# LayerNorm and tanh-weight FFN on 8 cores: square root moved from ScalarE to Newton steps on VectorE, weight loads issued one by one

## What is computed

```python
def _L0_attn_ref(x):                       # x: (1, 8192, 4096); b = 1
    q = jnp.transpose(x, (2, 0, 1))
    scores = jnp.einsum('lnc,lmc->lnm', q, q) / scale
    prob = jax.nn.softmax(scores, axis=-1) # over an axis of length 1: all ones
    msg = jnp.einsum('lnm,lmc->lnc', prob, q)
    return x + jnp.transpose(msg, (1, 2, 0))

x = x + _L0_attn_ref(_layernorm(x, axis=-1))
w_b = aa * jnp.tanh(kk * weight)           # weight: (4096, 4096)
x = x + jnp.einsum('bsi,oi->bso', _layernorm(x, axis=-1), w_b) + bias
```

## Time and profile before

| | us |
|---|---|
| timed runs | 626.97 and 639.13, median 633.05 |
| profiled execution | 626.53 |
| its span, slowest core | 625.0 |
| PE busy | 494.1 (79%) |
| ACT busy | 210.8 (34%) |
| DVE busy | 150.2 (24%) |
| chain that ended last | DMA 49%, PE 23%, ACT 9% |

### The profile page before, as it was taken

How to read it: one execution, slowest core, us unless ns; L and a number is a source line. 1 busy time by engine, 2 the same in 40 slices (tenths; PEclk the granted TensorE clock), 3 DMA queues, 4 the chain that set the end, 5 groups by cost and what they waited for, 6 DMA issues and landing times.

```text
span 625.0 us, 6936 instructions; the slowest of 8 cores (608.6 to 625.0 us)
## 1 busy us (share of the span) xinstructions
PE 494.1 (79%) x2335; PEld 230.9 (37%) x2379; DVE 150.2 (24%) x336; ACT 210.8 (34%) x228; POOL 83.5 (13%) x118
## 2 busy tenths in 40 slices
PE   3033467554388999999999957998999599989993
PEld 3021133231244444444444423443444244434441
DVE  0800245631882211120023003200230023022111
ACT  0255577763544433045004521352023312330000
POOL 0001000020001120212020302020202021212111
PEclk9556686688598999999999987999999989999998
DMA  7948846389654689999989999999877997899843
GB/s 192 287 163 247 290 172 242 126 189 301 236 131 102 190 229 228 233 285 288 228 152 285 278 196 236 241 257 251 141 221 218 239 276 220 223 280 207 171 94 80
DMA packets 47699, 134.72 MB, mean 216 GB/s; under 512 B 5680, under 2 KB 5680, under 8 KB 46640
## 3 DMA queue, kind: packets, MB, share of 16 engines
q0 software_dynamic: 16416, 43.00, 35.2%
q1 hardware_dynamic: 20016, 50.37, 24.4%
q10 hardware_dynamic: 11232, 40.90, 21.5%
HBM read 117.47 MB, written 16.78 MB: 215 GB/s over the span
## 4 chain that ended last, share of the span: by engine, by line
DMA 49%; PE 23%; ACT 9%; issue 5%; ACTq 5%; DVE 4%; POOL 2%; SPq 1%; DVEq 0%; POOLq 0%
DMA wring<-w2d 26%; PE ps_acc L323 20%; DMA outs<-biasrow 11%; DMA rb<-x 7%; ACT wp L235 6%; DMA xs<-x 5%; PE ps_tr L300 3%; ACT h2T L257 3%; ACTq L225 2%; ACTq L217 2%; POOL outs L354 1%; POOL wring L342 1%; DVE outs L148 1%; DVE stats L160 1%; ACT L246 1%
## 5 line engine op out<-in xcount | busy, mean ns | idle before, releaser
L323 PE MATMUL ps_acc<-wp,h2T 128*128 128x512 bf16 x2004 | 456.0, 388 | 46.0 <-ACT wp L235 31.2
L323 PEld LDWEIGHTS ps_acc<-wp,h2T 128*128 128x128 bf16 x2048 | 203.3, 100 | 296.6 <-issue 67.7
L235 ACT ACTIVATE wp<-wring,kk_sb 128x1024 bf16<-128x1024 f32 x128 | 141.1, 1141 | 266.2 <-DMA wring<-w2d 245.3
L148 DVE SCALAR_TENSOR_TENSOR outs<-rb,s1a,ps_acc 128x512 f32<-128x512 f32 x64 | 47.8, 747 | 350.5 <-DMA rb<-x 259.3
L354 POOL DMA_DIRECT2D outs<-biasrow x64 | 56.4, 1069 | 269.7 <-DVE outs L152 259.3
L300 PE MATMUL ps_tr<-ident_sb,h2b 128*128 128x128 bf16 x256 | 31.1, 280 | 46.1 <-DVE h2b L196 33.4
L342 POOL DMA_DIRECT2D wring<-w2d x50 | 28.6, 606 | 265.7 <-ACT wp L235 250.3
L160 DVE BATCH_NORM_STATS2 stats<-xs 128x6 f32<-128x512 f32 x64 | 38.7, 679 | 32.2 <-DMA xs<-x 32.2
L300 PEld LDWEIGHTS ps_tr<-ident_sb,h2b 128*128 128x128 bf16 x256 | 21.1, 121 | 57.8 <-issue 54.6
L257 ACT CAST h2T<-ps_tr 128x512 bf16<-128x512 f32 x64 | 34.2, 585 | 19.4 <-PE ps_tr L300 18.8
L152 DVE TENSOR_SCALAR outs<-outs,b1a 128x512 f32<-128x512 f32 x64 | 31.8, 497 | 5.3 <-issue 0.4
(11 more groups left out here) (20 smaller groups left out, 24.3 us busy)
## 6 DMA issues: line engine op xcount, KB each, us to landing
wring<-w2d ACTq DMA_DIRECT2D x78, 512.0 KB, 8.1
wring<-w2d POOLq DMA_DIRECT2D x50, 512.0 KB, 6.5
xs<-x SPq DMA_DIRECT2D x8, 2048.0 KB, 12.4
rb<-x SPq DMA_DIRECT2D x64, 256.0 KB, 9.2
outs<-biasrow POOLq DMA_DIRECT2D x64, 256.0 KB, 9.0
y<-outs SPq DMA_DIRECT2D x64, 256.0 KB, 7.4
ident_sb<-ident SPq DMA_DIRECT2D x1, 32.0 KB, 2.9
kk_sb<-kk SPq DMA_DIRECT2D x1, 0.5 KB, 2.3
```

The source lines that it names most:

```text
L148: vector.scalar_tensor_tensor(outs[g % 4][:, :], rbb[g % 4][:, :], s1a[:, t:t + 1], ps_acc[g % 4][:, :], ALU.mult, ALU.add)
L235: scalar.activation(wp[ot % 2][:, jop * WPC:(jop + 1) * WPC], wr[:, sl * WPC:(sl + 1) * WPC], AF.Tanh, bias=0.0, scale=kk[:, :]).then_inc( ...
L323: mm = tensor.matmul(ps_acc[g % 4][:, :], h2T[:, t * D + ic * 128: t * D + (ic + 1) * 128], wp[ot % 2][:, ic * 512:(ic + 1) * 512], start= ...
```

## The change

The square root leaves ACT. DVE forms 1/sqrt(v) itself: a first value 1/(0.5 + 0.5 v) and two Newton steps, all on columns of 128x1. ACT no longer takes part before h2b, and `s_sc` counts two steps a tile, not three. DVE gets two waits that ACT's turn gave before: ahead of the scalars until ACT has normalized its half of the tile before, and ahead of h2b until the transposes of the tile before are done. Independent of this, ACT drains after every tanh and issues the load for the freed slot at once; `flush_w` is gone.

```diff
--- before.py
+++ after.py
@@ -103,7 +103,7 @@
         sync.dma_start(xs[1][:, :], x_h[128:256, :]).then_inc(s_xin[1], 16)
 
         def load_x(t):
-            sync.wait_ge(s_sc, 3 * (t - 2) + 3)
+            sync.wait_ge(s_sc, 2 * (t - 2) + 2)
             sync.wait_ge(s_v, 4 * (t - 2) + 4)
             sync.dma_start(xs[t % 2][:, :], x_h[t * 128:(t + 1) * 128, :]).then_inc(s_xin[t % 2], 16)
 
@@ -163,9 +163,19 @@
             vector.bn_aggr(mv[:, 0:2], stats[:, 48 * p:48 * p + 48])
             vector.drain()
             vector.tensor_scalar(sc[:, 1:2], mv[:, 1:2], EPS, None, ALU.add).then_inc(s_v, 1)
-            vector.wait_ge(s_sc, 3 * t + 1)
+            vector.drain()
+            vector.tensor_scalar(sc[:, 0:1], sc[:, 1:2], 0.5, 0.5, ALU.mult, ALU.add)
+            vector.drain()
             vector.reciprocal(sc[:, 2:3], sc[:, 0:1])
             vector.drain()
+            for _ in range(2):
+                vector.tensor_scalar(sc[:, 3:4], sc[:, 2:3], sc[:, 2:3], sc[:, 1:2],
+                                     ALU.mult, ALU.mult)
+                vector.drain()
+                vector.tensor_scalar(sc[:, 3:4], sc[:, 3:4], -0.5, 1.5, ALU.mult, ALU.add)
+                vector.drain()
+                vector.tensor_mul(sc[:, 2:3], sc[:, 2:3], sc[:, 3:4])
+                vector.drain()
             vector.tensor_scalar(s1a[:, t:t + 1], sc[:, 2:3], 2.0, 1.0, ALU.mult, ALU.add)
             vector.scalar_tensor_tensor(b1a[:, t:t + 1], mv[:, 0:1], -2.0, sc[:, 2:3],
                                         ALU.mult, ALU.mult)
@@ -187,12 +197,16 @@
                 vector.drain()
             vector.tensor_mul(sc[:, 3:4], sc[:, 2:3], aa[:, :])
             vector.drain()
+            if t > 0:
+                vector.wait_ge(s_sc, 2 * t)
             vector.tensor_mul(sc[:, 6:7], s1a[:, t:t + 1], sc[:, 3:4])
             vector.scalar_tensor_tensor(sc[:, 7:8], mv[:, 0:1], -1.0, s1a[:, t:t + 1],
                                         ALU.mult, ALU.mult)
             vector.drain()
             vector.tensor_mul(sc[:, 7:8], sc[:, 7:8], sc[:, 3:4]).then_inc(s_v, 1)
             vector.drain()
+            if t > 0:
+                vector.wait_ge(s_trT, 8 * t)
             vector.tensor_scalar(h2b[:, 0:1024], xs[p][:, 0:1024], sc[:, 6:7],
                                  sc[:, 7:8], ALU.mult, ALU.add).then_inc(s_v, 1)
             vector.tensor_scalar(h2b[:, 1024:2048], xs[p][:, 1024:2048], sc[:, 6:7],
@@ -218,15 +232,6 @@
                              w_h[ot * 128:(ot + 1) * 128, j * WPC:(j + 1) * WPC]).then_inc(s_wl[sl], 16)
             wl[0] = w + 1
 
-        pend = [0]
-
-        def flush_w():
-            if pend[0]:
-                scalar.drain()
-                for _ in range(pend[0]):
-                    issue_w()
-                pend[0] = 0
-
         def tanh_batch(ot, lo=0, hi=NTO):
             for jop in range(lo, hi):
                 w = ot * NW + jop
@@ -235,16 +240,11 @@
                 scalar.activation(wp[ot % 2][:, jop * WPC:(jop + 1) * WPC],
                                   wr[:, sl * WPC:(sl + 1) * WPC],
                                   AF.Tanh, bias=0.0, scale=kk[:, :]).then_inc(s_wp, 1)
+                scalar.drain()
                 if sl < 3:
-                    pend[0] += 1
-                    if pend[0] == 3:
-                        flush_w()
-            flush_w()
+                    issue_w()
 
         def tile_block(t):
-            scalar.wait_ge(s_v, 4 * t + 1)
-            scalar.activation(sc[:, 0:1], sc[:, 1:2], AF.Sqrt).then_inc(s_sc, 1)
-            scalar.drain()
             scalar.wait_ge(s_v, 4 * t + 2)
             if t > 0:
                 scalar.wait_ge(s_trT, 8 * t)
@@ -289,9 +289,9 @@
                 elif k == 2:
                     tensor.wait_ge(s_v, 4 * t + 4)
                 elif k == 4:
-                    tensor.wait_ge(s_sc, 3 * t + 2)
+                    tensor.wait_ge(s_sc, 2 * t + 1)
                 elif k == 6:
-                    tensor.wait_ge(s_sc, 3 * t + 3)
+                    tensor.wait_ge(s_sc, 2 * t + 2)
                 trg = trg_ctr[0]
                 if trg >= 2:
                     tensor.wait_ge(s_evT, trg - 1)
```

## The result

The changed kernel takes 645.44 us (median of 11 runs, 642.49 to 650.94), the kernel before 631.34 in the same runs. The ratio is 1.025, 95% interval 1.021 to 1.029: slower, where 610 and a gain of 16 us were forecast. The profiled execution took 645.33 us, on its slowest core, core 4, a span of 643.8.

A forecast was written before the change was run, and what follows sets the result against it. The head was taken as bound by ACT's per-tile loop, with the PE idle, the tail by a loop through GpSimd. From 626.5 us, 13.7 + 1.5 - 0.3 + 1.5 = 16.4 came off, giving 610.1, range 602 to 617.

The forecast's parts named there:

- 28.0 forecast: Head, tiles 2 and 3: two tiles at 14.0 us each instead of 37.85 together, 9.9 us won.
- as taken: Batch 0 of tanh in the head: 1.5 us won, bounds 0.5 lost to 4 won.
- 110 and 138 forecast: Signs in the head: first bias accumulation at about 110 us, statistics of tile 5 at about 138.
- DVE's new waits: Head: waits before the last scalars and h2b give the old order's guarantee; cost 0.
- rival A: Head: x loads of tiles 3 and 4 replace the square root as limit, time 618; chance 0.18 together with rival D.
- rival D: Head: the square root was not on the path, only waits change place, 625; chance 0.18 together with rival A.
- The head terms: Head: 13.7 us won in tiles 1 to 3, 1.5 in batch 0, 0.3 lost in tile 5.
- one for one: Head: whatever brings the tanh at 123.33 us forward brings tile 5 forward equally; that tanh was to start 13.7 earlier.
- Tile 5 pays about +0.3 us: Head, tile 5: 1.9 us more DVE work for the root, less 1.68 us of waiting removed.
- 0.25 us won a block, 1.5 in all: Tail's tanh bursts: earlier weight issues against added drains, between -2 and +2 us for each of six blocks.
- the stretch from there to the last matmul keeps its length, give or take 10 us: Tail, from tile 7's first transposes on: length unchanged within 10 us, while those transposes come 15 us earlier.
- Rival B: Tail: earlier weight loads lengthen bias accumulations and rb reloads, 4 us in each of six blocks, 24 lost, 634; chance 0.08.

The follow-up runs named there:

- root only: Changed kernel with the kernel before's gathered weight issues (three loads behind one drain), so only the square root's move and its waits are new; 648.36 us, ratio 1.047.
- bias rows: Bias given as 128 equal rows instead of one row read 128 times: root only 587.78 us, full change 584.39, kernel before 602.95.
- the issues alone: Kernel before with a drain and one weight issue after each tanh, square root still on ACT; 611.03 us, ratio 0.986.
- full kernel: The whole change, square root on DVE and weight loads issued one by one, against the kernel before; 645.44 us, ratio 1.025.
- the one root at the end: One square root of a constant, read by nobody, added after ACT's last tanh: root only 619.35 us, ratio 0.975; full change 605.37 us, ratio 0.950.
- the moved row: Root only with the bias in row 37 of 64 equal rows, still read 128 times; 620.01 us, ratio 0.975.
- the four-core run: Root only launched on four cores, meant as one of each pair but numbered 0 to 3 in the profile; 643.9 us.

## Why the prediction was wrong

**Right, with sizes.** The mechanism of the head held: the root off ACT shortens its loop. Two tiles take 27.0 us (28.0 forecast). Batch 0 on ACT ran from 39.2 to 65.6, 26.4 us against 27.9: 1.5 won, as taken. The first bias accumulation came at 103.9 and tile 5's statistics at 134.5 (110 and 138 forecast). DVE's new waits cost nothing: tile 2's scalars waited 18.73 us for ACT and its h2b 5.12 us for the transposes, and it was still written by 75.8, where the PE wanted it at 82.07. The statistics of tiles 3 and 4 did wait for x, 2.27 and 3.11 us, which the prediction named as the sign of rival A; it cost nothing, for their transposes followed the group before without a stop. The head terms sum to 14.9 us; measured were 12.7 in the mean of the cores, 14.2 on a single core (root only), 15.5 with bias rows. That the sum comes so near is in part luck. In the mean of the cores tile 3's first tanh came 19.6 us earlier (122.0 to 102.4), where 15.2 were forecast: batch 0 began 1.7 us earlier, which the sum did not count, and every later step won a little more. Of that 4.4 us were lost on the way to tile 5's statistics (148.2 to 133.1, 15.2 earlier), so "one for one" did not hold, and 2.5 more behind them. The price of a table load was the row's 1.28 and not more: before, the first tanh began 1.32 us after the last cast's end (84.16, 85.48); now the last cast ends at 73.72 + 1.08 = 74.80 and the tanh at 74.69 overlaps it. By ScalarE: Activation LUTs of the Trainium skill ("What ACT_TABLE_LOAD costs", some 1380 ns of drain beside each load) more should have come back; the trace does not bear the drain out here.

**Mis-sized: Newton steps in tiles 5 to 7.** "Tile 5 pays about +0.3 us", and nothing was put down for tiles 6 and 7. DVE sets the pace there: statistics to statistics 161.14 - 148.00 = 13.1 us. Before, tiles 6 and 7:

```profile
166.33 4.84 DVE L160 BATCH_NORM_STATS2 stats<-xs 128x6 f32<-128x512 f32 x8
...
177.83 4.85 DVE L160 BATCH_NORM_STATS2 stats<-xs 128x6 f32<-128x512 f32 x8
```

That is 11.5 us. From tile 5's statistics to the end of the head it is 178.6 - 134.5 = 44.1 us, against 194.7 - 153.6 = 41.1: 3 us, not 0.3.

**Mis-sized: the tail's bursts.** "0.25 us won a block, 1.5 in all" for one-by-one issues does not show where nothing else lengthens the tail: with bias rows it is 395.0 with them and 394.7 without. With one bias row the tails differ by 14.7 us with the issues alone, 9.4 between the root-only and the full kernel when both have the one root at the end (419.0 to 409.6), and by nothing between the root-only and the full kernel as they are. Each of these is another program, and one dead instruction moves the tail by 27 us, so how much of 14.7 or 9.4 belongs to the issues is not shown.

**Failed: the tail carries over.** The sum took it that "the stretch from there to the last matmul keeps its length, give or take 10 us". It grew by 28.8 us in the mean and 35 on the slowest core. Rival B named the right place and nearly the right size (24 us, for 634), by longer accumulations and reloads, but the wrong cause: it blamed the early weight issues, without which the tail is as long. The cause has two parts. The first is shown: it takes a single bias row read 128 times per accumulation and at least one other core running; alone or with 128 rows the tail is 395, with other cores and one row 403 to 455 in the mean of the cores. The second is shown in its effect: how much is lost depends on whether the program holds a Sqrt, not on when it runs. One dead root gives root only a ratio of 0.975, and the full change 0.950. That it acts through where things lie in memory is argued from the moved row, which gives root only 0.975 too. None of the rows of the kernel before shows this. A hint was there in 20.98 us for the accumulation of 256 KB in the earlier trace rows, a single one: over the whole span the median of the accumulations was 9.0 us and that of the equally large rb reloads 9.2.

The change itself does what was argued when the row is out of the way: with bias rows 584.39 against 602.95, in the same set of runs, 0.919 / 0.948 = 0.970, a gain of 3%.

**Open.** What the bias row meets at its bad place (the other core's row, a table, instructions or another tensor) was not found. Where tensors were placed is not in the trace, nor does a view put two cores on one clock, so that they meet on the row in time is argued: that a core's tensors lie elsewhere when a second core is launched would fit the runs on one and two cores too. Bias rows on one core, and the larger y on eight, were not run. Whether the second core must share the memory stack is open, since the four-core run could not be assigned; six more cores, at any rate, add nothing to what two show (445.9 against 454.9).

## What to carry to other kernels

When a change moves the time of a stretch whose instructions it didn't touch, run both kernels on one core and on two before looking for a mechanism in the order of work; then add dead work and see whether the effect follows time or follows the program's contents. Until that is known, a difference of a few per cent between two variants may belong to neither edit. A small constant that every transfer reads again, such as a bias broadcast over partitions from one row, is worth spreading over rows when all cores run: here it gave 5% to the old kernel and 10% to the new one, and left a tail of 395 us whatever was done with the root and the issues.

## What the runs showed of the hardware

A dead ACT instruction after the last use of ACT took a kernel from a ratio of 1.047 to 0.975 (tail 445.9 to 419.0), and moving its bias row within an enlarged tensor did the same (tail 417.3). Where one 2 KB row was read 128 times per transfer, a core alone had a tail of 395.0 or 395.4, the same as with 128 rows; with other cores running the mean tails were 8 to 60 us longer, though single cores went from 394.7 to 462.5. HBM Reference of the Trainium skill ("Specifications (TRN2)") says that the two cores of a pair share a stack's bandwidth and that a DMA-bound change should be timed with the pair active; the runs agree that a second core decides: the root's move is worth -14.0 us on one core and +24.7 on cores 0 and 1 together (single runs). In the tail the cost is no fixed share of bandwidth, for with bias rows eight cores ran it as fast as one. In the head other cores still cost time with bias rows: root only has a head of 156.2 us alone and 174.5 with eight.
